# A graph-network kernel: two query weights folded into one on the chip, and zero columns of weights in place of memsets

## What is computed

```python
for n in range(STEPS):                    # 2 steps
    q = Xa @ W1.T @ W2.T                  # W1: 64x128, W2: 64x64
    k = Xa @ W3.T                         # W3: 64x128
    probs = softmax(q @ k.T)              # 2048 x 2048
    A = probs * mask                      # keeps the largest up to a mass of 0.9
    A = A / max(A.sum(-1), 1e-12)
    Xf = R @ Xf
    Xa = A @ Xa
    Z = Z + Xf @ U1[n].T + Xa @ U2[n].T
```

## Time and profile before

| | |
|---|---|
| median of 3 runs | 1067.96 us (1066.7 to 1069.11) |
| profiled execution, first to last instruction | span 1063.4 us |
| PE busy | 838.8 us (79%) |
| VectorE busy | 779.5 us (73%) |
| ScalarE busy | 510.0 us (48%) |
| GpSimd busy | 69.7 us (7%) |
| chain that ended last, by engine | PE 46%, DVE 27%, ACT 13%, issue 9%, POOL 2%, DMA 1% |
| mean granted TensorE clock | 0.899 of full |

### The profile page before, as it was taken

The page is one execution under the profiler, slowest core; times in us unless marked ns, Lnnn a source line. Parts: engine busy times, 40 slices in busy tenths (PEclk is TensorE's granted clock), DMA queues, the critical chain, the costliest instruction groups (busy, mean ns, idle before and its releaser), DMA issues.

```text
span 1063.4 us, 12286 instructions
## 1 busy us (share of the span) xinstructions
PE 838.8 (79%) x3886; PEld 566.1 (53%) x3886; DVE 779.5 (73%) x2363; ACT 510.0 (48%) x979; POOL 69.7 (7%) x68
## 2 busy tenths in 40 slices
PE   5889958887887853939779878868658999996695
PEld 4844425655665642737256557547447475553342
DVE  5968779888987998971697899889789702326715
ACT  4877235357368376413552664674775232023212
POOL 0020110000000000000000000010001100002201
PEclk9899998998988995969799789989789999998798
DMA  9849304424004000000043320230260456500001
GB/s 339 344 174 431 119 8 151 132 106 159 1 1 159 1 0 2 1 2 1 1 158 124 108 88 1 79 136 1 59 269 15 153 238 253 221 1 0 1 0 40
DMA packets 20221, 108.25 MB, mean 102 GB/s; under 512 B 1824, under 2 KB 8752, under 8 KB 9776
## 3 DMA queue, kind: packets, MB, share of 16 engines
q1 hardware_dynamic: 18752, 106.77, 27.0%
q10 hardware_dynamic: 1392, 0.61, 0.2%
HBM read 88.23 MB, written 19.14 MB: 101 GB/s over the span
## 4 chain that ended last, share of the span: by engine, by line
PE 46%; DVE 27%; ACT 13%; issue 9%; POOL 2%; DMA 1%; DVEq 1%; POOLq 0%; SPq 0%; ACTq 0%
PE PS L808 10%; DVE AT L1520 8%; PE PS L743 6%; PE PS L676 5%; PE PS L546 5%; DVE mxv L1659 4%; PE PS L877 3%; ACT BC L1249 3%; ACT AT L1249 3%; DVE nd L1523 3%; PE PS L1060 3%; PE PS L1036 3%; PE PS L1066 2%; DVE AT L2106 2%; ACT AT L1082 2%
## 5 line engine op out<-in xcount | busy, mean ns | idle before, releaser
L1082 ACT ACTIVATE AT<-PS 128x512 f32<-128x512 f32 (+2 forms) x240 | 118.8, 561 | 121.3 <-PE PS L546 103.7
L743 PE MATMUL PS<-K,ST 128*128 128x512 f32 x224 | 125.6, 713 | 13.0 <-ACT EA L1217 7.6
L546 PE MATMUL PS<-ident,AT 128*128 128x128 f32 x544 | 85.5, 293 | 55.4 <-DVE rS L2161 24.5
L1520 DVE SCALAR_TENSOR_TENSOR AT<-EA,se 128x2048 uint8<-128x2048 f32 (+1 forms) x46 | 107.6, 2345 | 1.6 <-DVE se L1513 0.3
L546 PEld LDWEIGHTS PS<-ident,AT 128*128 128x128 f32 x544 | 68.7, 152 | 64.0 <-DVE rS L2161 26.1
L1520 DVE SCALAR_TENSOR_TENSOR AT<-AT 128x2048 uint8<-128x2048 f32 (+2 forms) x48 | 96.1, 2002 | 2.0 <-PE PS L546 1.1
L1659 DVE TENSOR_REDUCE mxv<-PS 128x1 f32<-128x2048 f32 x32 | 73.3, 2289 | 26.0 <-PE PS L743 20.4
L743 PEld LDWEIGHTS PS<-K,ST 128*128 128x128 f32 x224 | 49.4, 232 | 73.1 <-issue 73.0
L2106 DVE MAX8 AT<-AT 128x8 f32<-128x256 f32 x256 | 87.6, 412 | 0.7
L808 PE MATMUL PS<-hr,AT 128*128 128x128 f32 x512 | 69.8, 285 | 9.2 <-ACT AT L1082 8.4
L808 PE MATMUL PS<-AT 128*128 128x128 f32 x512 | 68.3, 281 | 8.7 <-ACT AT L1082 8.1
(11 more groups left out here) (297 smaller groups left out, 1473.1 us busy)
## 6 DMA issues: line engine op xcount, KB each, us to landing
AT<-keep_at SPq DMA_DIRECT2D x32, 1024.0 KB, 5.1
EA<-in_adj SPq DMA_DIRECT2D x20, 1024.0 KB, 6.8
keep_at<-AT SPq DMA_DIRECT2D x8, 2048.0 KB, 24.9
AT<-keep_at SPq DMA_DIRECT2D x8, 2048.0 KB, 12.3
AT<-in_adj SPq DMA_DIRECT2D x12, 1024.0 KB, 5.0
EA<-keep_degrees SPq DMA_DIRECT2D x1, 1024.0 KB, 6.5
keep_x<-K SPq DMA_DIRECT2D x4, 256.0 KB, 8.6
out<-EA SPq DMA_DIRECT2D x4, 256.0 KB, 2.3
```

What stands on the lines that cost most here:

```text
L546: return pe.transpose(dst, src, ident[0:p, 0:p])
L743: mm = pe.matmul(bank(half(gi, k) + n), ST[1][:, k * P:(k + 1) * P], wide_keys[:, n * BK:(n + 1) * BK], start=True, stop=True)
L1082: return act.activation(dst, src, ACT.Copy)
L1520: return dve.scalar_tensor_tensor(out=o, in0=x0, scalar=s, in1=x1, op0=op0, op1=op1, **k)
```

## The change

W1 and W2 are multiplied once, on the chip, and every query is one product. The folded weight `QT` is 128 columns wide: the left half is the product, the right half is written by ScalarE as the same PSUM data times 0. The turned W3 is written twice, side by side, so the keys come out in all 128 partitions (the lower half repeats the upper). Queries therefore have zeros in partitions 64 to 127 by the product itself, and what stands in the keys there does not count; no memset and no `zero_ok` remain. One turn of a weight goes (W1 is used as it is), and the six `wt_ok` of the start now are two copies of W3, then W2 and the rest; two more come behind the folding product (`qw_mm`). That product stands on PE between the wait for the six and the first L676. `first_query` moves from inside the b = 3 loop to behind `first_rows(NB - 1)`. Copies of keys and queries, `ksum` and the means cover 128 partitions.

```diff
@@ -48,7 +48,7 @@
-W1T, W3T, W2T, U1T, U2T, L2WT, L3WT = 0, 1, 2, 3, 5, 7, 8
+QT, W3T, W2T, U1T, U2T, L2WT, L3WT = 0, 1, 2, 3, 5, 7, 8
@@ -128,8 +128,7 @@
-        keys = K[0:DA, :, :].rearrange("p t c -> p (t c)")
-        wide_keys = K[:, :, :].rearrange("p t c -> p (t c)")
+        keys = K[:, :, :].rearrange("p t c -> p (t c)")
...
@@ -450,27 +449,9 @@
             n += 2
-            def keys_zeroed(b, count):
-
-                pool.wait_ge(x1_dma[b], 16)
-                if count > 0:
-                    pool.wait_ge(zero_ok, count)
-                pool.memset(K[DA:P, b * G:(b + 1) * G, :], 0.0).then_inc(zero_ok, 1)
-
-            for b in range(NB - 1):
+            for b in range(NB):
                 power(sm[:, 3, :], sm[:, 2, :], 0, G, n + 1 + b)
-            pool.wait_ge(pw_out, n + NB - 1)
-            for b in range(NB - 1):
-                keys_zeroed(b, b)
-            pool.wait_ge(ps_t, 1 + NB)
-            pool.wait_ge(zero_ok, NB - 1)
-            pool.memset(ST[1][DA:P, :], 0.0).then_inc(zero_ok, 1)
-            pool.wait_ge(zero_ok, NB)
-            power(sm[:, 3, :], sm[:, 2, :], 0, G, n + NB)
             n += NB
-            pool.wait_ge(pw_out, n)
-            keys_zeroed(NB - 1, NB)
-            pool.wait_ge(zero_ok, NB + 1)
             power(esc[:, :], cs[:, :], 1, NT, n + 1)
@@ -575,7 +556,6 @@
-            turn(bank(4)[:, 0:DA], raw[0:DA, 0, :])
@@ -637,6 +617,7 @@
             pe.wait_ge(wt_ok, 6)
+            pe.matmul(bank(3)[:, 0:DA], raw[0:DA, 0, :], WT[0:DA, W2T, 0:DA], start=True, stop=True).then_inc(qw_mm, 1)
@@ -652,21 +633,15 @@
                 pe.wait_ge(h_st, 1 + NB + n + 1)
-                pe.matmul(bank(n)[0:DA, :], WT[:, W3T, 0:DA], XT[:, n * BK:(n + 1) * BK],
-                          start=True, stop=True).then_inc(k_mm, 1)
+                pe.matmul(bank(n), WT[:, W3T, :], XT[:, n * BK:(n + 1) * BK], start=True, stop=True).then_inc(k_mm, 1)
...
-                pe.matmul(bank(7)[0:DA, :], WT[:, W1T, 0:DA], XT[:, 0:BK], start=True, stop=True).then_inc(t1_mm, 1)
-
-            def second_query():
-
-                pe.wait_ge(t1_out, 1)
-                pe.matmul(bank(7)[0:DA, :], WT[0:DA, W2T, 0:DA], ST[0][0:DA, :], start=True, stop=True)\
-                  .then_inc(q_mm, 1)
+                pe.wait_ge(wt_ok, 8)
+                pe.matmul(bank(7), WT[:, QT, :], XT[:, 0:BK], start=True, stop=True).then_inc(q_mm, 1)
             MEANWHILE = {3: lambda: first_rows(2), 4: lambda: hr_turned(0), 5: lambda: hr_turned(1),
-                         7: lambda: keys_of(0), 8: lambda: keys_of(1), 9: first_query}
+                         7: lambda: keys_of(0), 8: lambda: keys_of(1)}
             for b in range(NB):
...
@@ -704,11 +679,7 @@
                     pe.wait_ge(un_z, issued)
-                pe.matmul(bank(7)[0:DA, :], WT[:, W1T, 0:DA], src[:, g * BK:(g + 1) * BK], start=True, stop=True)\
-                  .then_inc(t1_mm, 1)
-                pe.wait_ge(t1_out, gi + 1)
-                pe.matmul(bank(7)[0:DA, :], WT[0:DA, W2T, 0:DA], ST[0][0:DA, :], start=True, stop=True)\
-                  .then_inc(q_mm, 1)
+                pe.matmul(bank(7), WT[:, QT, :], src[:, g * BK:(g + 1) * BK], start=True, stop=True).then_inc(q_mm, 1)
@@ -720,12 +691,12 @@
-                                   ST[1][0:DA, k * P:(k + 1) * P], ksum[0:DA, :], start=True, stop=True)
+                                   ST[1][:, k * P:(k + 1) * P], ksum[:, :], start=True, stop=True)
...
-            def logit_part(k, n):
-
-                return pe.matmul(bank(4 * k + n), ST[1][:, k * P:(k + 1) * P], wide_keys[:, n * BK:(n + 1) * BK],
+            def logit_part(to, k, n):
+
+                return pe.matmul(bank(to + n), ST[1][:, k * P:(k + 1) * P], keys[:, n * BK:(n + 1) * BK],
@@ -740,9 +711,7 @@
-                    mm = pe.matmul(bank(half(gi, k) + n), ST[1][:, k * P:(k + 1) * P],
-                                   wide_keys[:, n * BK:(n + 1) * BK],
-                                   start=True, stop=True)
+                    mm = logit_part(half(gi, k), k, n)
@@ -881,38 +850,35 @@
                 pe.wait_ge(exT_ok, G * (n + 1))
-                pe.matmul(bank(n)[0:DA, :], WT[:, W3T, 0:DA], xaT[:, n * BK:(n + 1) * BK],
-                          start=True, stop=True).then_inc(k_mm, 1)
+                pe.matmul(bank(n), WT[:, W3T, :], xaT[:, n * BK:(n + 1) * BK], start=True, stop=True).then_inc(k_mm, 1)
...
                     pe.wait_ge(q_out, 1)
-                    pe.wait_ge(zero_ok, NB)
                     for n in range(3):
                         pe.wait_ge(k_out, n + 1)
-                        logit_part(0, n)
+                        logit_part(0, 0, n)
                         if n < 2:
-                            logit_part(1, n)
+                            logit_part(4, 1, n)
                     hr_turned(3)
...
                     pe.wait_ge(k_out, 4)
-                    pe.wait_ge(zero_ok, NB + 1)
-                    logit_part(0, 3).then_inc(logits_ok, 1)
+                    logit_part(0, 0, 3).then_inc(logits_ok, 1)
                     means(0, 0)
-                    logit_part(1, 3)
+                    logit_part(4, 1, 3)
                     pe.wait_ge(mean_ok, 1)
-                    logit_part(1, 2).then_inc(logits_ok, 1)
+                    logit_part(4, 1, 2).then_inc(logits_ok, 1)
                     for k in range(2, G):
...
                     pe.wait_ge(k_out, NB + 4)
-                    logit_part(0, 3).then_inc(logits_ok, 1)
+                    logit_part(0, 0, 3).then_inc(logits_ok, 1)
                     means(1, 0)
                     for n in (0, 1, 3):
-                        logit_part(1, n)
+                        logit_part(4, 1, n)
                     pe.wait_ge(mean_ok, NB + 1)
-                    logit_part(1, 2).then_inc(logits_ok, 1)
+                    logit_part(4, 1, 2).then_inc(logits_ok, 1)
                     for k in range(2, G):
@@ -1110,14 +1076,17 @@
             act.wait_ge(wt_t, 1)
-            copy(WT[:, 0, 0:DA], bank(4)[:, 0:DA]).then_inc(wt_ok, 1)
-            copy(WT[:, 1, 0:DA], bank(4)[:, P:P + DA]).then_inc(wt_ok, 1)
+            for h in range(2):
+                copy(WT[:, W3T, h * DA:(h + 1) * DA], bank(4)[:, P:P + DA]).then_inc(wt_ok, 1)
             copy(WT[0:DA, 2, 0:DA], bank(4)[0:DA, 2 * P:2 * P + DA]).then_inc(wt_ok, 1)
...
             copy(ST[1][0:NT, 0:P], bank(2)[0:NT, 0:P]).then_inc(deg_s, 1)
+            act.wait_ge(qw_mm, 1)
+            copy(WT[:, QT, 0:DA], bank(3)[:, 0:DA]).then_inc(wt_ok, 1)
+            act.activation(WT[:, QT, DA:P], bank(3)[:, 0:DA], ACT.Copy, scale=0.0).then_inc(wt_ok, 1)
@@ -1141,8 +1110,8 @@
                 act.wait_ge(k_mm, 4 * step + n + 1)
-                act.activation(keys[:, n * BK:(n + 1) * BK], bank(n)[0:DA, :], ACT.Copy,
-                               accum_out=ksum4[0:DA, n:n + 1]).then_inc(k_out, 1)
+                act.activation(keys[:, n * BK:(n + 1) * BK], bank(n), ACT.Copy,
+                               accum_out=ksum4[:, n:n + 1]).then_inc(k_out, 1)
@@ -1154,12 +1123,10 @@
                 keys_of(0, n)
-            act.wait_ge(t1_mm, 1)
-            copy(ST[0][0:DA, :], bank(7)[0:DA, :]).then_inc(t1_out, 1)
             first_out(NB - 1)
...
             act.wait_ge(q_mm, 1)
-            copy(ST[1][0:DA, :], bank(7)[0:DA, :]).then_inc(q_out, 1)
+            copy(ST[1][:, :], bank(7)).then_inc(q_out, 1)
             for n in range(2, NB):
@@ -1169,11 +1136,8 @@
                 gi = NB * step + g
-                act.wait_ge(t1_mm, gi + 1)
-
-                copy(ST[0][0:DA, :], bank(7)[0:DA, :]).then_inc(t1_out, 1)
                 act.wait_ge(q_mm, gi + 1)
-                copy(ST[1][0:DA, :], bank(7)[0:DA, :]).then_inc(q_out, 1)
+                copy(ST[1][:, :], bank(7)).then_inc(q_out, 1)
@@ -2169,7 +2133,7 @@
                 dve.wait_ge(k_out, 4 * (step + 1))
-                total(ksum[0:DA, :], ksum4[0:DA, :]).then_inc(ksum_ok, 1)
+                total(ksum[:, :], ksum4[:, :]).then_inc(ksum_ok, 1)
                 row_maxima(NB * step)
...
                 guess_first(NB * step)
```

More of the change, by code:

```diff
@@ L223, in rows @@
             return PS[:, b, :].rearrange("p (k c) -> p k c", c=P)
-        names = """in_x in_small ident_ok expo_ok wt_t wt_ok nat_sum nat_act at_t at_out pw_in pw_out h_ready h_t h_st
+        names = """in_x in_small ident_ok expo_ok wt_t wt_ok qw_mm nat_sum nat_act at_t at_out pw_in pw_out h_ready h_t h_st
             s_mm s_out nd_ok deg_t deg_s deg_d1 deg_d2 y_ok ps_mm ps_st ps_t ps_u ps_row ps_z z_dma
-            sums x1_ok late_in dve_steps act_steps pool_steps k_mm k_out t1_mm t1_out q_mm q_out
+            sums x1_ok late_in dve_steps act_steps pool_steps k_mm k_out q_mm q_out
             logits_ok negmax_ok exp_ok round_steps kept_ok e_turned e_copied ex_mm ex_ok
@@ L684, in _ @@
             first_rows(NB - 1)
-            second_query()
+            first_query()
             keys_of(2)
```

8 lines of the change are left out of this document (4 added, 4 removed).

## The result

The changed kernel takes 1102.6 us at the median (1097.1 to 1107.6 over four runs), the kernel before 1067.4 beside it (1066.7 to 1069.1): a ratio of 1.032, with a 95% interval of 1.028 to 1.037. I had forecast 1061.6, and that is 41 us off. The profiled execution is the second shortest of the four, 1098.2 us; its span is 33.1 us longer than before.

What follows compares the result with a forecast made beforehand. No engine bounds the kernel; the chain passes between TensorE, VectorE and ScalarE. Terms +0.3 - 1.83 - 2 x 1.7 - 0.39 - 0.70 - 0.35 give -6.4 us: 1061.6 us, range 1058.8 to 1065.6.

Steps and rivals of the forecast that it cites:

- slower rival: Folding rounds queries otherwise, so a group takes VectorE's branch: 8.3 us of flag loads plus unpriced passes, 1070 us or more; chance 0.03.
- the tail: More gain than seen, from a wait wrongly taken for tied (the fifth query's 3 us): -9.4 us, 1058.6 us; chance 0.05.
- The main case: The summed terms, -6.4 us (bounds -5.0 to -7.0), time 1061.6 us, 1060 to 1064 with run spread; chance 0.70.
- start, 61 to 83 us: Before the first products: one transpose goes, the folding product with its tile-size change comes in; +0.3 us, bounds 0 and +0.6.
- keys and first query: Inside the b = 3 products: wide keys stop a 0.34 us loss per visit and the query leaves the loop; net -1.83 us.
- sixth query: The path runs through both products to the row maximum at 532.63, before which VectorE was idle 0.70 us: -0.70 us.
- seventh query: More time is freed, but VectorE was only 0.43 us idle, of which 0.04 is handover: -0.39 us.
- Fourth and eighth query: ScalarE starts its threshold sums earlier by a saved copy, under VectorE's idle time of 2.65 and 2.74 us: -1.7 us each.
- The other rule, on the load time: A skill page's rule that load time grows with columns: full-width keys cost 53 ns more a load, making the sum 0.9 us smaller.
- given back: A later wait may swallow both 1.7 us terms of the fourth and eighth query: -3.0 us in all, 1065.0 us; chance 0.12.
- Clock: Low TensorE clock in the unit's products behind the second and sixth query returns 5 us: -1.4 us, 1066.6 us; chance 0.10.
- It doesn't do what it says: Memsets are worth 0 anyway; if the narrow tile is not the cost, -5.4 us, 1062.6 us, inside the main range.

Runs made afterwards that it cites:

- e5: Kernel before with only the outer flag set by hand in the groups of queries 7 and 8, so the branch looks but cuts no tile: 1082.8 us against 1067.0.
- e4: Kernel before with flags set by hand in the groups of queries 7 and 8, forcing the branch with one tile cut each: 1109.2 us against 1067.7.
- e3: Changed kernel with the test for exact ties left out of the branch flag, so no branch is taken: 1063.3 us, ratio 0.9968 to the kernel before.
- e8: The same kernel as e3, run again to see why its times spread: 1065.1 us (1056.1 to 1068.9), ratio 0.9973 to the kernel before.
- e1: Changed kernel without the folding, queries made by two products as before; wide keys, zero columns and no memsets stay: 1066.6 us against 1067.7 for the kernel before.

## Why the prediction was wrong

**The step that failed is the slower rival's chance and price, and with them a term that the sum lacks.** The sum has the branch at nothing; it was taken in two groups and cost 23.6 and 17.6 us. The mechanism was written down as it came: other rounding of the queries, an exact comparison, a branch, flags loaded more than 32 times. I gave it 0.03, on the ground that "eight of eight groups" of the trace were clear of it. That is no evidence on how near the groups of this data are to a tie: the same eight groups, scaled by 1.1 instead, have one. In twelve roundings six had a tied group. The eight looks told what the kernel before had drawn, not what a new draw brings. Its price was 8.3 us for the loads of one group, with the passes on top unpriced. In the seventh group it is 11.4 us for the looks (e5), since a look costs 2.3 us and not the 1.7 of its loads, and 12 us for the passes and the scan, 23.3 together (e4); in the last group 17.7 are left of 30.8 (e4). A small slip beside it: the range ends at 1058.8, and so leaves out the 1058.6 of the tail that it is said to take in.

**The main case, term by term.** With the ties ignored (e3 and e8) the terms can be read from the shifts of VectorE's instructions. The times are those of before. The three columns are three profiled executions; the changed kernel's own is valid up to its first tie.

```
term                        forecast    changed    e3      e8
start, 61 to 83 us           +0.3       +1.99    +0.31   +0.30
keys and first query         -1.83      -1.88    -1.89   -1.88
second, third query           0         -0.51    -0.46   -0.43
fourth query                 -1.7       -1.70    -1.69   -1.70
behind it, by 371 us          -         +1.63    +1.63   +1.64
keys of step 1, fifth query  -0.35      -0.47    -0.31   -0.38
sixth query                  -0.70      -0.79    -0.77   -0.77
behind it, by 564 us          -         +0.45    +0.47   +0.52
seventh query                -0.39      -0.39    -0.39   -0.39
behind it, by 631 us          -         -2.05    -2.04   -2.03
eighth query                 -1.7       -1.72    -1.71   +1.58
behind it, by 713, 735 us     -         -0.39    -0.39   -0.40
by 751 us                     -         -1.43    -1.43   +0.12
sum                          -6.4       -7.3     -8.7    -3.8
```

The changed kernel is 0.5 us ahead already at 61 us, before anything the diff touches, which makes its -7.3 the -7.8 above; e3 is 0.8 ahead there and e8 0.5. Behind the second of the two 1.7 us terms 1.7 us return as well; they stand under "713, 735 us", after 2.06 gained there. Of the row "second, third query" 0.22 us fall at 134 us and are the memset's.

In e3 the rows for which I had a number other than 0 add up to -6.45 us, where I had -6.4. The rows that I had at 0 or did not have add up to another -2.2, made of 2.1 lost and 4.3 gained, so that their sum is no larger is luck.

*Start*: +0.3 as forecast, where the clock stays up. In the changed kernel it doesn't. By stretch (busy time of the engines, then the granted clock), 65 to 70 us, the changed kernel and e3, which run the same instructions there:

```profile
65.00:70.00 5.00, 5.00 (x10) 2.15 (x10) 4.86 (x5) 4.01 (x5) 1.54 (x1) 0.66 0.59 131
```

```profile
65.00:70.00 5.00, 5.00 (x12) 2.28 (x13) 4.86 (x4) 4.29 (x7) 1.26 (x1) 1.00 0.65 129
```

The granted clock is 0.66 in the one and 1.00 in the other, and 1.7 us lie between them. e4 has this too, at 0.57, with before's own code up to there. So it is no price of the folding product. Ten of the eighteen profiled executions, of either kind, have a clock of 0.50 to 0.68 in this stretch, the other eight 1.00.

*Keys and first query*: right to 0.06 us, and for the reason given. A key pair and the L651 pair behind it take 0.86 us each in the changed kernel (117.22, 118.08, 118.94, 119.80), against the earlier trace rows. The Trainium skill, "TensorEngine Tiling (Array Packing)", section Key Properties, says that a change of tiling mode drains TensorE; the trace agrees in so far as a pass pair of another mode in the stream costs 0.34 us, there and back; a drain as such it does not show. The other rule, on the load time, would have made this term 0.9 us smaller, and no such cost shows here.

```profile
117.22 1.02 PE L636 MATMUL PS<-XT,WT 128*128 128x512 f32 x2
118.08 1.02 PE L651 MATMUL PS<-AT,R 128*128 128x512 f32 x2
118.94 1.02 PE L636 MATMUL PS<-XT,WT 128*128 128x512 f32 x2
119.80 6.17 PE L651 MATMUL PS<-AT,R 128*128 128x512 f32 x14
```

*Fourth and eighth query*: 1.7 each as forecast (in e8 the eighth's is hidden behind the low stretches at 630 and 658 us), VectorE's idle time before it reads the sums is 0.96 and 1.03 us now (of before: the earlier trace rows).

```profile
320.71 0.16 DVE L1484 SCALAR_TENSOR_TENSOR se<-below,se 128x4 f32<-128x4 f32 x1 [0.96 <-ACT BC L1213]
679.28 0.16 DVE L1484 SCALAR_TENSOR_TENSOR se<-below,se 128x4 f32<-128x4 f32 x1 [1.03 <-ACT BC L1213]
```

But the forecast stopped at the first wait behind each query, and the next one matters as much. Behind the fourth query VectorE waits 1.56 us for logits where it had waited 0.04, and 1.63 us are given back, in all three executions: the "given back" rival, at one of its two places. (At the other, behind the eighth, the like happens at 735 us, 1.56 us of wait instead of 0.22, but with 2.1 gained ahead of it and, where the clock stays up, 1.43 behind it.) Against that, behind the seventh a wait of 1.95 us for TensorE goes, for TensorE had itself stood 2.20 us for ScalarE's exponential (0.26 now); that this is ScalarE's freed copy is argued from the order of its program, but e1, which keeps both copies, has no such gain. I had written off all of the seventh query's freed time but 0.39 because VectorE's first wait was that short.

*Clock*: at the second query the rival came in the changed kernel's own profile, and not in e3's or e8's. TensorE stands 1.90 us for VectorE's mean, and the unit's products behind it start at the low clock (granted clock 0.66 between 170 and 175 us, 1.00 in e3), the thirty passes taking 7.75 us where they took 6.64:

```profile
171.18 0.90 PE L592 MATMUL PS<-AT,hr 128*128 128x256 f32 x2 [1.90 <-DVE gs L1481]
172.72 7.75 PE L592 MATMUL PS<-AT,hr 128*128 128x256 f32 x30
172.82 6.64 PE L612 MATMUL PS<-AT,hr 128*128 128x256 f32 x30
```

The last line is the kernel before. At 203 us another low stretch (0.77 between 200 and 205 us, before 0.98) makes VectorE wait 1.35 us longer. Neither lasts: by 304 us it is 0.29 us further ahead than at the first row maximum, which is why the table's row shows nothing of it. At the sixth query it did not come. Where the clock did cost was elsewhere: from 61 to 751 us the best profile gains 8.7 us and the other 3.8 with the same code. By the times of e3 and e8 the change without its ties is worth 0.3% (ratios 0.9968 and 0.9973), some 3 us, not 6.4; by the medians alone it is 4.4 and 1.9. What the forecast couldn't see, the ties apart, was how often the low stretch falls onto the path, and the waits behind the first one.

*It doesn't do what it says*: the memsets and wide keys by themselves bring nothing that can be measured (e1, 0.9982 to 1.0002). The folding is what gains, and what loses. (The memsets, priced at 0, were 0.22 us on the path, too little to show in the time.)

## What to carry to other kernels

A change that touches rounding ahead of an exact comparison draws the data-dependent path anew. Count how often the trace of before was clear of the branch only as one draw; get the odds by perturbing the rounding at no cost, such as a factor on one weight and its inverse on the other, and price the taken branch by forcing it once. And follow freed time past the first wait behind it: a short wait there does not end the account, since the engine that releases the next one may have been freed as well.

## What the runs showed of the hardware that I had not expected

A look of four register loads on VectorE costs 2.3 us of an idle engine (five in 11.44 us, e5), 0.6 more than the sum of the loads (0.42 each), and nothing ran on it beside them. Not taking the branch seems to have a price as well: ahead of the last group's masks VectorE is idle for 6.32 us in the kernel before, which jumps over the branch, and for 2.15 in the changed kernel, which goes in, with the same four loads ahead. Inside the branch of the last group the 3.6 us between two looks stand at a jump as well, over the exact search that was not needed; the same jump in the seventh group took 1.0. That the jump is the cause was not tested, and what makes the two groups differ is open.

```profile
840.33 2.35 DVE L1520 SCALAR_TENSOR_TENSOR AT<-AT,s 128x2048 f32<-128x2048 f32 x1 [6.32 <-issue]
```

A memset of 64x512 on GpSimd, 0.52 us, slows the VectorE passes that run beside it: two of the four take 0.63 and 0.49 us instead of 0.29 and 0.28, and 0.2 us is lost in all.

And one program can spread over 10 us, 1%, from run to run (e3; 13 in e8, and 10 in the changed kernel) where its predecessor spreads over 3 to 4; the longer runs are those with the lower mean granted clock.
